# Moving the slot reduction behind the routing logits, putting all eight PSUM copies of the transposed input on VectorE, and moving the bias preamble behind the first layer norm

## The reference, cut to what matters

```python
xn = _layernorm(x)
# ssm: three projections, a gated linear recurrence over the tokens, a projection
w, k = (xn @ Wp + bp)[..., 0:1024], (xn @ Wp + bp)[..., 1024:2048]
u = xn @ Wu + bu
gate = sigmoid(w)
s_t = gate * (s * tanh(k) + u) + (1 - gate) * s
ssm = s @ Wo + bo
# slots: route every token to 8 of 64 slots
ctx = concat([xn, mean(slot_init)])
h = gelu(ctx @ w1 + b1)
logits = (h @ w2 + b2) / (abs(tau) + 0.1)
alpha = softmax over the top 8 logits, zero elsewhere
slot_input = alpha.T @ xn ; denom = alpha.sum(tokens)
# GRU cell, attention among 64 slots, layer norm -> slot_values (64 x 1024)
slots = alpha @ slot_values @ wo + bo
```

## Time and profile before

| what | us |
|---|---|
| time, median of 3 runs (lowest to highest) | 1858.41 (1854.53 to 1930.88) |
| the profiled execution: its time / its span | 1860.1 / 1858.6 |
| spans of the eight cores | 1839.6 to 1858.6 |
| PE matmul busy | 1530.6 (82%) |
| DVE busy | 726.2 (39%) |
| ACT busy | 606.7 (33%) |
| pass 1, from the first matmul of `wku_loop(0)` to the last of `wo_block(15)` | 107.9 to 1348.8 |

### The profile page before, as it was taken

One profiled execution on the slowest core, in us unless ns is written; L12 is line 12 of the kernel. 1 busy time (PEld: TensorE's weight loads), 2 busy tenths in 40 slices (PEclk: granted clock), 3 DMA queues, 4 the chain that ended last, 5 costly groups with the idle time before them and its releaser, 6 DMA issues.

```text
span 1858.6 us, 20925 instructions; the slowest of 8 cores (1839.6 to 1858.6 us)
## 1 busy us (share of the span) xinstructions
PE 1530.6 (82%) x7221; PEld 672.1 (36%) x7221; DVE 726.2 (39%) x1295; ACT 606.7 (33%) x990; POOL 26.9 (1%) x54
## 2 busy tenths in 40 slices
PE   0198989889898898989889898898944369999998
PEld 0043434434344443434444344443411123333332
DVE  0134546354463634546354463544610312222222
ACT  0252534535344352533525344252201121111110
POOL 0100000000000000000000000000011000000000
...
DMA packets 42679, 166.52 MB, mean 90 GB/s; under 512 B 4290, under 2 KB 5458, under 8 KB 41682
## 3 DMA queue, kind: packets, MB, share of 16 engines
...
HBM read 128.68 MB, written 67.11 MB: 105 GB/s over the span
## 4 chain that ended last, share of the span: by engine, by line
PE 70%; DMA 10%; DVE 7%; issue 5%; ACT 4%; DVEq 3%; ACTq 0%; SPq 0%; POOL 0%; POOLq 0%
PE psA L1045 8%; PE psA L498 6%; PE psA L502 6%; PE psC L507 6%; PE psC L502 6%; PE psB L498 6%; PE psB L507 6%; PE psA L569 5%; PE psA L352 4%; PE psC L1045 3%; PE psB L1045 3%; PE psB L569 3%; DMA sb_b_c<-b_pk 3%; DVEq L102 2%; ACT sb_xn_f L480 2%
## 5 line engine op out<-in xcount | busy, mean ns | idle before, releaser
L538 DVE SCALAR_TENSOR_TENSOR sb_a_sb<-sb_g_sb,sb_s_sb 128x512 f32<-128x512 f32 x128 | 88.6, 692 | 295.6 <-ACT sb_s_sb L523 295.6
L1045 PE MATMUL psA<-sb_wo_sb,sb_z_f 128*128 128x512 bf16 x512 | 141.0, 438 | 20.3 <-ACT sb_z_f L1014 18.6
L550 DVE TENSOR_TENSOR_SCAN sb_ys_bf<-sb_a_sb,sb_ys_bf,sb_b_sb 128x512 bf16<-128x512 f32 x120 | 154.0, 1283 | 9.1
L352 PE MATMUL psA<-sb_Wo_sb,sb_ys_bf 128*128 128x512 bf16 x512 | 121.6, 387 | 27.8 <-DVE sb_x_sl L380 27.8
L1060 DVE TENSOR_TENSOR sb_prd<-psA,sb_prd 128x1024 f32<-128x1024 f32 x32 | 39.2, 1224 | 258.0 <-DMA sb_prd<-out 163.8
L480 ACT ACTIVATE sb_xn_f<-psT 128x512 bf16<-128x512 bf16 x64 | 38.2, 597 | 294.0 <-PE psT L465 294.0
L19 ACT ACT_TABLE_LOAD x83 | 106.5, 1283 | 81.7 <-PE psA L569 65.1
L498 PE MATMUL psA<-sb_xn_f,sb_Wp_sb 128*128 128x512 bf16 x512 | 122.6, 383 | 0.0
L1014 ACT ACTIVATE sb_z_f<-psC 128x512 bf16<-128x512 f32 x64 | 35.7, 630 | 263.9 <-PE psC L1006 263.9
L502 PE MATMUL psA<-sb_xn_f,sb_Wp_sb 128*128 128x512 bf16 x512 | 121.2, 380 | 0.0
L502 PE MATMUL psC<-sb_xn_f,sb_Wp_sb 128*128 128x512 bf16 x512 | 121.0, 379 | 0.0
...
## 6 DMA issues: line engine op xcount, KB each, us to landing
...
```

Source lines behind the costliest of these rows:

```text
L352: P.op("pe", lambda e, i=i, f=f, k=k, ps=ps: e.matmul(ps[:, f * 512:(f + 1) * 512], t.ys_bf[:, k, i * 128:(i + 1) * 128], t.Wo_sb[:, k, f ...
L538: P.op("ve", lambda v, pp=pp: v.scalar_tensor_tensor(t.a_sb[:], t.g_sb[:, pp, :], -2.0, t.s2_sb[:, pp, :], ALU.mult, ALU.mult))
L550: P.op("ve", lambda v, j=j, init=init: v.tensor_tensor_scan(t.ys_bf[:, j, :], t.a_sb[:], t.b_sb[:], init, ALU.mult, ALU.add), inc="sve", e ...
L1045: P.op("pe", lambda e, i=i, f=f, k=k, ps=ps, p2=p2: e.matmul(ps[:, f * 512:(f + 1) * 512], t.z_f[:, p2 % 2, k, i * 128:(i + 1) * 128], t.w ...
```

## The change

There are four edits.

1. The preamble for `bias_h`, with the loads of Wo, wq and wk behind it, moves as it is to behind `ln_apply(0)`.
2. In `xn_transposes` all eight copies to `xn_f` are made by DVE; ACT makes none.
3. `wku_loop` and `h_logits` wait only for the last copy (one engine now makes them in order).
4. In the phase loop `slot_pe(ph-1)` and `slot_ve(ph-1)` move from ahead of `xn_transposes(ph)` to behind `h_logits(ph)`.

```diff
@@ preamble: the whole block from here to the gload2 loads is moved to behind ln_apply(0)
-    P.wait_all_dma("pe", ("cload",), "sx")
-    P.wait_all_dma("pe", ("wload",), "sg")
-    pe_claim("T0")
...
-    for i, fn in enumerate(gload2):
-        P.dma("gp", fn, "sg", event=("wload2",) if i == len(gload2) - 1 else None)
@@ xn_transposes
-            eng = "ve" if k % 2 == 0 else "se"
-            P.wait(eng, ("xnT", ph, k))
+            P.wait("ve", ("xnT", ph, k))
             if ph >= 1 and k < 2:
-                P.wait(eng, ("wku", ph - 1, ND - 1))
-                P.wait(eng, ("hmm", ph - 1, NH - 1))
-            if k % 2 == 0:
-                P.op("ve", lambda v, k=k, psT=psT: v.tensor_copy(
-                    t.xn_f[:, k, :], psT[:, 0:Tp]), inc="sve",
-                    event=("xnf", ph, k))
-            else:
-                P.op("se", lambda s, k=k, psT=psT: s.activation(
-                    t.xn_f[:, k, :], psT[:, 0:Tp], AF.Identity), inc="sse",
-                    event=("xnf", ph, k))
+                P.wait("ve", ("wku", ph - 1, ND - 1))
+                P.wait("ve", ("hmm", ph - 1, NH - 1))
+            P.op("ve", lambda v, k=k, psT=psT: v.tensor_copy(
+                t.xn_f[:, k, :], psT[:, 0:Tp]), inc="sve", event=("xnf", ph, k))
             release(reg, ("xnf", ph, k))
@@ wku_loop and h_logits
         P.wait("pe", ("xnf", ph, ND - 1))
-        P.wait("pe", ("xnf", ph, ND - 2))
@@ phase loop
+        if ph < NPH:
+            xn_transposes(ph)
+            h_logits(ph)
         if ph >= 1:
             slot_pe(ph - 1)
             slot_ve(ph - 1)
         if ph < NPH:
-            xn_transposes(ph)
-            h_logits(ph)
             wku_loop(ph)
```

More of the change, by code:

```diff
@@ L206, in build_walk @@
         out=t.bo_tot[:], in_=t.bo1_r[:]), "sg", event=("botot",))
-    P.wait_all_dma("pe", ("cload",), "sx")
-    P.wait_all_dma("pe", ("wload",), "sg")
-    pe_claim("T0")
[L211 to L245, removed]
-                ps4[jh][:, 0:1], t.w1s[:, k % 2, jh * 128:(jh + 1) * 128],
-                t.sm_fb[:, k:k + 1], start=(k == 0), stop=(k == ND - 1)),
-                inc="spe" if jh == NH - 1 else None,
-                event=("smwk", k) if jh == NH - 1 else None)
@@ L250, in build_walk @@
-    P.wait("ve", ("smwk", ND - 1))
-    for jh in range(NH):
-        P.op("ve", lambda v, jh=jh: v.tensor_add(
-            t.bias_h[:, jh:jh + 1], t.b1_c[:, jh:jh + 1], ps4[jh][:, 0:1]),
-            inc="sve" if jh == NH - 1 else None,
-            event=("biash",) if jh == NH - 1 else None)
-    for r in regs4:
-        release(r, ("biash",))
-    for i, fn in enumerate(gload2):
-        P.dma("gp", fn, "sg", event=("wload2",) if i == len(gload2) - 1 else None)
     def stats_tile(ph, i):
```

52 lines of the change are left out of this document (added).

## The result

| | before | after |
|---|---|---|
| median of the runs | 1857.12 us (8 runs) | 1896.75 us (8 runs, 1894.46 to 1898.75) |
| profiled execution, its span | 1860.1 us, 1858.6 us | 1897.1 us, 1895.6 us |
| phase, mean of 8 cores and 15 phases | 78.6 us | 80.9 us |

The ratio is 1.0212, with a 95% interval of 1.0199 to 1.0225: slower by 2.1%. The prediction was +11.3 us and the result is +39.6 us, inside the range. The direction was right and the size was not.

What follows compares the result with a forecast made beforehand. PE (82% busy) was taken as the engine to follow. +0.62 us a phase (1.36 plain, -0.74 clock) is +9.3 us in 15 phases; with +2 us preamble, +11.3 us, so 1870 us median; range 1846 to 1904 us.

Steps and rivals of the forecast that it cites:

- The stretch ahead of the logits: From the last Wo tile's end to the logits matmuls: about 6 us after the change, starting them 3.7 us sooner.
- The three costs behind the logits: On PE each phase: wait for ACT's C0 copy 0.87 us, slot matmuls 2.19, wait for B0 2.00; together 5.06 us.
- The plain sum: Each phase without the clock: 5.06 us added less 3.7 us gained, so 1.36 us longer.
- The preamble: Before the first phase: first logits matmul at 97.8 us instead of 95.72, +2 us once.
- The clock: PE's fall to half clock: logits block 4.6 us instead of 5.34, -0.74 us a phase; nothing for the stretch behind.
- The third one: Rival: the new stretch behind the logits falls to half clock, 1909 to 1920 us if in every phase; chance 0.17.
- The 15 x 3.3 us of the recorded sum: Third rival's price over 15 phases, on top of 1870 us, giving 1920 us.
- the 0.62 us: Forecast net lengthening of each phase, plain sum and clock together; +9.3 us in 15 phases.
- the bound of 37 us: 2% of the run time; within it a measurement of this kernel tells nothing from no change.
- The first (the clock takes it up): Rival: shorter half-clock stretches keep the phase's length, leaving only the preamble's +2 us: 1860 us; chance 0.2.
- The second (no fall ahead of the logits): Rival: logits block at full clock, 3.6 us, phase 0.4 us shorter: 1854 us, perhaps 1846; chance 0.15.

Runs made afterwards that it cites:

- the last kernel: Kernel before, with all eight copies on DVE, alpha copied out of T1 first and the slot sums behind the eight copies: 1810.06 us, ratio 0.9722.

## Why the prediction was right and wrong

- **The stretch ahead of the logits** was forecast at 6.0 us and took 6.34. The copies take 0.42 us and DVE keeps up, as the row had said. By the Trainium skill, VectorE: DVE Perf Modes, section Rules for kernel authors, it would have been one element per cycle, an estimated 0.66 us; the traces do not agree with that for a bf16 copy out of PSUM (0.42 us, and 0.76 us for two, in the last kernel). The estimate of 0.66 us came from the Trainium skill, VectorE: DVE Perf Modes, section on the TRN2 errata, where the elements are divided by a perf-mode multiplier, which the prediction left out; with 2 it gives an estimate of 0.39 us, near the trace. An fp32 copy of 64x512 out of PSUM does take 0.67 us (before, the slot sum of phase 0, at 168.07).
- **The three costs behind the logits** were forecast at 5.06 us and took 5.15 us, in the parts named: 0.98 (0.87), 2.2 (2.19), 1.93 (2.00). So "the wait for `slot_ve` does not go: it moves from T1 to B0" holds.
- **The plain sum** of +1.36 us a phase was +1.2 us. **The preamble** was +2 us; the first logits matmul comes at 97.95 instead of 95.72 us, 2.2 us later.
- **The clock** is the step that failed. The term was -0.74 us a phase, and it had two parts. For the logits block I had taken 4.6 us, since the dense matmuls start 3.7 us sooner; on the slowest core it mostly stayed at 5.3 to 5.9 us, and its share of the clock part fell by only 0.24 us. Starting sooner did not make the block shorter where the clock fell; what little was gained comes from the phases in which it did not fall there. For the stretch behind the logits the term was nothing: I had written "I take nothing for it in the sum and give it a rival of its own". It took 1.5 us. The argument against it, that 2.00 us at T1 "mostly pass without a fall", was misread: the wait itself passes at 1.00, but the fall comes 2.3 us after it, at 964.84, and the logits matmuls pay in 118 of 120 phases of before. Together the term was +1.1 us (+1.3 us on the slowest core of each, 3.75 less 2.45): 15 x 1.1 = 17 us in place of -11, which is 28 us, about the whole miss of 28.3 us.
- **The rivals.** The third one, a fall in the new stretch behind the logits, is what happened, in its place, in 92 of 120 phases, but at 1.5 us a phase rather than the 3.2 to 5.1 us that I had priced from two odd phases. Those two were another case: both had a last Wo tile at the low clock (5.24 and 5.30 us) and a logits block of 6.17 and 6.47 us, and the first projections were slow only in the second (3.32 us for eight, at 664.29). The 15 x 3.3 us of the recorded sum doesn't follow from them either: 4.2 us less the 0.62 us is 3.6. It was to decide when it cost over 1.8 us a phase; at 1.5 us, and with the 0.74 us of the logits block mostly not earned, the median came out just beyond the bound of 37 us (the profiled execution at it). The first (the clock takes it up) did not occur: the falls went up from 16 to 25 in 15 phases. The second (no fall ahead of the logits) did in part: the first 16 logits matmuls ran at full clock in 26 of 120 phases, and in 2 of 120 before. The Trainium skill, TensorE: Matmul & The Clock Gate, section A second HAM failure mode: psum-queue depth-cycling, was the rule that spoke for the third. The trace agrees in part: the second fall comes behind two short idles at the claims of C0 and B0, 0.91 and 1.93 us, with a few matmuls between them, and without them (the kernel with neither wait) the projections run at 379 ns a matmul. But there the fall still comes in 57 of 120 phases, in the slot matmuls.

The trace of before had the like of it: the sparse stretch of some 10 us ahead of the logits costs 1.74 us of clock in each phase. A second stretch of 5 us with two waits in it deserved a price of that order in the sum, and not zero with a rival beside it. That the result fell inside the range is owed to the width of the range, which ran up to the third rival.

What stays open: why the fall comes 1 us into the dense projections and not in the waits, why the logits block changes when only what stands behind it is changed (1.0 to 1.9 us in the table), and how the clock part would have to be computed beforehand. Taking one wait away removed 1.3 us of it, taking the other away 0.4 us, and taking both away 0.9 us, so these don't add up, and no run here says why.
